# Cross-attention stage of a Perceiver layer: DMA order, the 65-row tile's sum, and the order of work at a step's end

## The reference, cut to what matters

```python
C_q  = layernorm(x) @ Wq_d;  C_kv = ctx @ Wkv_d          # 1601 keys of 32 latents per batch
scores = einsum('bnhl,bkl->bhnk', (C_q @ W_qk) by head, C_kv) / sqrt(32)
attn = softmax(scores);  V_up = C_kv @ Wv_u               # 16 heads of 32
x = x + einsum('bhnk,bkhd->bnhd', attn, V_up)
# beside it, for later blocks:
k_sel, v_sel = k_cache[block_idx], v_cache[block_idx]     # 16 of 128 blocks
coeff = mean(abs(w - mean_w))                             # for w1, w3 and w2
```

## Time and profile before

| | us |
|---|---|
| median of 3 runs | 1012.36 (1009.2 to 1012.99) |
| the profiled execution | 1013.66 |
| its span | 1011.9 |
| TensorE busy | 916.1 (91%) |
| VectorE, ScalarE, GpSimd busy | 619.5, 509.6, 384.4 |

### The profile page before, as it was taken

How to read it: one execution, slowest core, us unless ns; L and a number is a source line. 1 busy time by engine, 2 the same in 40 slices (tenths; PEclk the granted TensorE clock), 3 DMA queues, 4 the chain that set the end, 5 groups by cost and what they waited for, 6 DMA issues and landing times. The chain is left out here.

```text
span 1011.9 us, 15312 instructions
## 1 busy us (share of the span) xinstructions
PE 916.1 (91%) x5330; PEld 660.0 (65%) x5330; DVE 619.5 (61%) x994; ACT 509.6 (50%) x995; POOL 384.4 (38%) x256
## 2 busy tenths in 40 slices
PE   4748999999599897999999999999999997699997
PEld 2324454444344376888888888888888886578886
DVE  2444467556365154767757576775757675598783
ACT  2314566655455454645636364563636554255551
POOL 2024578656555502433423243342323332244430
PEclk9956999999699889999999999999999998889999
DMA  9475855534430062101101010110101000355531
GB/s 324 185 234 205 300 159 218 176 132 147 155 110 1 1 250 94 42 22 42 42 21 54 29 41 21 41 41 21 53 30 41 12 1 1 124 188 191 206 104 41
DMA packets 46178, 103.70 MB, mean 102 GB/s; under 512 B 11314, under 2 KB 16434, under 8 KB 45106
## 3 DMA queue, kind: packets, MB, share of 16 engines
q1 hardware_dynamic: 44754, 102.94, 29.6%
q10 hardware_dynamic: 1376, 0.13, 0.1%
HBM read 97.08 MB, written 1.05 MB: 97 GB/s over the span
## 5 line engine op out<-in xcount | busy, mean ns | idle before, releaser
L1324 POOL TENSOR_TENSOR head_probs<-head_probs,inverse_den 128x576 f32<-128x576 f32 x128 | 146.8, 1147 | 297.7 <-DVE inverse_den L1255 297.6
L806 DVE TENSOR_REDUCE max_part<-psum 128x1 f32<-128x804 f32 x128 | 121.4, 990 | 85.0 <-PE psum L608 84.9
L741 ACT ACTIVATE probs<-psum 128x512 f32<-128x512 f32 (+1 forms) x208 | 108.7, 600 | 51.3 <-PE psum L629 45.3
L1202 ACT ACTIVATE head_probs<-psum,neg_max 128x576 f32<-128x576 f32 x128 | 94.5, 738 | 76.7 <-PE psum L1093 43.1
L534 POOL TENSOR_TENSOR prob_sums<-probs 128x1024 f32<-128x1024 f32 x48 | 115.0, 2405 | 44.8 <-ACT probs L741 44.6
L1268 DVE TENSOR_REDUCE neg_max<-psum 128x1 f32<-128x576 f32 x128 | 96.2, 754 | 36.2 <-PE psum L1077 29.6
L608 PE MATMUL psum<-c_t,q_t 96*128 96x402 f32 x256 | 80.9, 405 | 19.7 <-DMA c_t<-c_high 13.9
L629 PE MATMUL psum<-q_t,c_t 97*128 97x512 f32 (+1 forms) x208 | 77.9, 448 | 19.6 <-ACT probs L741 18.1
L1248 DVE TENSOR_TENSOR probs_t_low<-psum,probs_t_high 128x512 fp32r<-128x512 f32 x128 | 87.5, 684 | 9.5 <-ACT probs_t_high L1208 8.4
L608 PEld LDWEIGHTS psum<-c_t,q_t 96*128 96x128 f32 x256 | 49.1, 211 | 62.1 <-DVE max_part L806 34.6
L1077 PE MATMUL psum<-k_high,query_t_high 128*128 (+1 forms) x256 | 84.2, 329 | 4.9 <-DVE query_t_low L1233 2.9
(11 more groups left out here) (161 smaller groups left out, 1909.8 us busy)
## 6 DMA issues: line engine op xcount, KB each, us to landing
cache<-in_ctx_dram SPq DMA_DIRECT2D x4, 3202.0 KB, 12.4
ctx_t_odd<-in_ctx_dram SPq DMA_DIRECT2D x4, 3202.0 KB, 14.3
w_raw<-in_L_ffn_w_dram SPq DMA_DIRECT2D x24, 448.0 KB, 5.1
w_raw<-in_L_ffn_mean_w_dram SPq DMA_DIRECT2D x24, 448.0 KB, 6.0
ffn_raw<-in_L_ffn_w_dram SPq DMA_DIRECT2D x42, 256.0 KB, 3.8
ffn_raw<-in_L_ffn_mean_w_dram SPq DMA_DIRECT2D x42, 256.0 KB, 4.1
wq_nat<-in_L_attn_wq_dram SPq DMA_DIRECT2D x32, 256.0 KB, 2.7
wo_nat<-in_L_attn_wo_dram SPq DMA_DIRECT2D x32, 256.0 KB, 2.6
```

Source lines behind the costliest of these rows:

```text
L741: act.activation(prob_buffer(b, t)[0:rows, half * BANK:(half + 1) * BANK], psum[0:rows, n % SCORE_BANKS, :], ACT.Exp, scale=XSCALE).then_i ...
L806: dve.tensor_reduce(max_part[:, qt, pair:pair + 1], psum[:, bank:bank + 2, 0:PIECE_KEYS], AX.XY, ALU.max).then_inc(s_max, 1)
L1202: act.activation(probs[:, qt, :].rearrange("p (a k) -> p a k", a=2), psum[:, 2 * (qt % 2):2 * (qt % 2) + 2, 0:HALF], ACT.Exp, bias=neg_max ...
L1324: pool.tensor_tensor(probs[:, qt, :], probs[:, qt, :], rden[:, qt:qt + 1].to_broadcast([P, KEYS]), ALU.mult).then_inc(s["norm"], 1)
```

## The change

The weight pieces get a semaphore for each of their three pairs, a load of pair i waits for the absolute sum of pair i alone, and a difference for its own pair. On SP, `place_keys(b)` stands ahead of the load of context b+2, and the cache gather behind the last pieces. GpSimd's `add_tail` adds the 65-row tile into the sixth sum, and the two matmuls on it go. `scores(b+1, 1)` stands ahead of `denominators(b)`, `scores(b, 3)` ahead of `mix(b-1)`, `copy_den` behind tile 1. The second and third absolute sum stand behind a step's last exponential. VectorE's addition to `x` (`add_mixed`) stands behind `negate_max`.

```diff
-ABS_AT = (3, 5, 7)
+ABS_AT = 3
...
-    s_raw = core.sem("w_raw_in", own)
+    s_raw = [core.sem(f"w_raw_in{i}", own) for i in range(3)]
...
-        return (g // KT) * ADDS + min((g % KT) // 2 + 1, ADDS) if g >= 0 else 0
+        return (g // KT) * (ADDS + 1) + (g % KT) // 2 + 1 if g >= 0 else 0
...
         @block.sync
-            def load_pieces(k):
-                wait(sp, s_abs, 3 * k)
-                for i, pair in enumerate(wnames):
-                    for j, n in enumerate(pair):
-                        sp.dma_start(w_raw[:, i, j, :], flat[n][:, k * PIECE:(k + 1) * PIECE]).then_inc(s_raw, 16)
+            def load_pieces(k, i):
+                wait(sp, s_abs, 3 * (k - 1) + i + 1)
+                for j, n in enumerate(wnames[i]):
+                    sp.dma_start(w_raw[:, i, j, :], flat[n][:, k * PIECE:(k + 1) * PIECE]).then_inc(s_raw[i], 16)
...
-            load_pieces(0)
+            for i in range(3):
+                load_pieces(0, i)
             sp.dma_start(index[:, :], arg["block_idx"].rearrange("(a k) -> a k", a=1)).then_inc(s_idx, 16)
             for b in range(BATCH):
+                if b > 2:
+                    load_pieces(b - 1, 1)
+                    load_pieces(b - 1, 2)
+                place_keys(b)
                 if b + 2 < BATCH:
                     sp.wait_ge(s_c, b + 1)
                     load_context(core, ctx_t, sp, b + 2, b % 2)
-                place_keys(b)
-                if b == BATCH - 2:
-                    sp.wait_ge(s_idx, 16)
-                    sp.wait_ge(s_c, BATCH - 1)
-                    gather_cache(core, sp, index)
-                if b > 0:
-                    load_pieces(b)
+                if b == 1:
+                    load_pieces(1, 0)
+                    load_pieces(1, 1)
+                    load_pieces(1, 2)
+                elif b > 1:
+                    load_pieces(b, 0)
+            load_pieces(BATCH - 1, 1)
+            load_pieces(BATCH - 1, 2)
+            sp.wait_ge(s_idx, 16)
+            gather_cache(core, sp, index)
...
         @block.gpsimd
-                pool.wait_ge(s_raw, 96 * (k + 1))
+                pool.wait_ge(s_raw[i], 32 * (k + 1))
...
+            def add_tail(b):
+                pool.wait_ge(s_exp, HALVES * (b + 1))
+                pool.wait_ge(s_add, (ADDS + 1) * b + ADDS)
+                pool.tensor_tensor(sums[ADDS - 1][0:TAIL, :], sums[ADDS - 1][0:TAIL, :],
+                                   prob_buffer(b, KT - 1)[0:TAIL, :], ALU.add).then_inc(s_add, 1)
...
                     add_pair(s, u)
                     if s == 0 and u == 0:
                         compressed_low(2)
+                add_tail(s)
                 if s + 3 < BATCH:
                     compressed_low(s + 3)
...
         @block.tensor
                 for k in range(ADDS // 2):
-                    pe.wait_ge(s_add, ADDS * b + 2 * k + 2)
+                    pe.wait_ge(s_add, (ADDS + 1) * b + (2 * k + 2 if k < ADDS // 2 - 1 else ADDS + 1))
...
-                for half in range(2):
-                    at = 2 * LKV * half + LKV
-                    mm = pe.matmul(psum[at:at + LKV, DEN_BANK, :], ones[0:TAIL, :],
-                                   prob_buffer(b, KT - 1)[0:TAIL, half * BANK:(half + 1) * BANK], start=False, stop=True)
                 mm.then_inc(s_den, 1)
...
                     scores(b, 2 * u + 2)
                     if lead:
                         max_scores(b + 1, 3 * u + 1 if u == 0 else 3 * u)
+                    if b == 0 and u == 0:
+                        compress(2)
+                    scores(b, 2 * u + 3)
                     if b > 0 and u == 0:
                         mix(b - 1)
-                    elif u == 0:
-                        compress(2)
-                    scores(b, 2 * u + 3)
...
                 if lead:
                     scores(b + 1, 0)
+                    scores(b + 1, 1)
                 denominators(b)
-                if lead:
-                    scores(b + 1, 1)
...
         @block.scalar
                         wait(act, s_add, pairs_summed(b, t))
-                        wait(act, s_den, tails_summed(b, t))
...
                     exponential(b, t)
-                    if t == 0 and b > 0:
+                    if t == 1 and b > 0:
                         copy_den(b - 1)
-                    if t in ABS_AT and b + 1 < BATCH:
-                        abs_sum(b + 1, ABS_AT.index(t))
+                    if t == ABS_AT and b + 1 < BATCH:
+                        abs_sum(b + 1, 0)
...
+                if b + 1 < BATCH:
+                    abs_sum(b + 1, 1)
+                    abs_sum(b + 1, 2)
                 if b + 3 < BATCH:
                     compressed(b + 3)
...
         @block.vector
                 mm.then_inc(s_mix, 1)
+
+            def add_mixed(b):
                 if b % 2:
                     dve.wait_ge(s_mix, b + 1)
...
                     negate_max(b + 1)
                 else:
                     update_x(b - 1)
+                if b > 0:
+                    add_mixed(b - 1)
                 if b + 3 < BATCH:
                     place_values(b + 3)
                 copy_u(b)
             update_x(BATCH - 1)
+            add_mixed(BATCH - 1)
```

More of the change, by code:

```diff
@@ L477, in pairs_summed @@
         g = KT * b + t - 4
-        return (g // KT) * ADDS + min((g % KT) // 2 + 1, ADDS) if g >= 0 else 0
-    def tails_summed(b, t):
-        g = KT * b + t - 4
-        return g // KT + 1 if g >= 0 and g % KT == KT - 1 else 0
+        return (g // KT) * (ADDS + 1) + (g % KT) // 2 + 1 if g >= 0 else 0
     with nc.Block() as block:
@@ L658, in denominators @@
                             at = 2 * LKV * half + LKV * odd
-                            pe.matmul(psum[at:at + LKV, DEN_BANK, :], ones[:, :],
-                                      sums[2 * k + odd][:, half * BANK:(half + 1) * BANK],
-                                      start=(k == 0), stop=(k == ADDS // 2 - 1 and odd == 0))
-                for half in range(2):
-                    at = 2 * LKV * half + LKV
-                    mm = pe.matmul(psum[at:at + LKV, DEN_BANK, :], ones[0:TAIL, :],
-                                   prob_buffer(b, KT - 1)[0:TAIL, half * BANK:(half + 1) * BANK], start=False, stop=True)
+                            mm = pe.matmul(psum[at:at + LKV, DEN_BANK, :], ones[:, :],
+                                           sums[2 * k + odd][:, half * BANK:(half + 1) * BANK],
+                                           start=(k == 0), stop=(k == ADDS // 2 - 1))
                 mm.then_inc(s_den, 1)
```

## The result

The changed kernel takes 977.51 us (median of 4 runs, 974.57 to 979.48), the kernel before, in the runs beside it, 1010.78 us (1008.8 to 1012.99). The ratio is 0.967 (95%: 0.963 to 0.971). Predicted were 981.5 us and a range of 975 to 990, which holds it. The profiled execution took 976.39 us, its span 974.6; before it was 1013.66 and 1011.9.

What follows compares the result with a forecast made beforehand. TensorE, 91% busy, was taken as the bound, with its waits and slow clock open to gain. 6.3 + 7.4 + 1.2 + 3.1 + 14.0 - 0.5 - 0.2 = 31.3 us gave 981.5 us, range 975 to 990.

Steps and rivals of the forecast that it cites:

- Part 1: Stage start: place_keys(0) ahead of context 2 brings the first max scores earlier, gain 6.3 us.
- Part 2: Start of each step: tile matmuls gone and scores 1 ahead of the sums, 1.05 us seven times, gain 7.4 us.
- part 3: Mid-step: GpSimd gets the denominators earlier, so its lag in steps 1 and 3 goes, gain 1.2 us.
- Part 4: Addition to x moved to a step's end: TensorE's wait for VectorE in steps 2, 4 and 6 goes, gain 3.1 us.
- Part 5: GpSimd's add_tail: one more instruction of 2.4 us a step, on the path only at step 7's end, cost 0.5 us.
- Part 6: Gather behind the pieces: the stall and slow clock in step 5 go, gain 14.0 us.
- Part 7: Two absolute sums behind the last exponential: 0.1 us each in steps 5 and 6, cost 0.2 us.
- Rival B: Step 7 stays at full clock despite its wait, some 3 us more gain, 978.5 us; chance 0.11.
- A: Start of each step: copy_den behind tile 1 eats the gain of the new order, 989 us; chance 0.12.
- D: Slower: the clock falls at a new wait and stays down within the step, 1034 us with four; chance 0.02.
- E: Pieces for step 5 still come late, as a load waits for a sum at a step's end, 995.5 us; chance 0.02.
- C: New waits drop the clock at the start of steps 1 to 6, 4.1 us each, 1006 us; chance 0.03.

Runs made afterwards that it cites:

- context_first: Changed kernel with the load of context b+2 ahead of place_keys(b) again; 985.84 us, ratio 0.977.
- tail_on_pe: Changed kernel without add_tail, the two matmuls on the 65-row tile back in the denominators on TensorE; 981.59 us, ratio 0.972.
- old_start: Changed kernel with scores 1 behind the denominators and copy_den behind tile 0 again; 985.17 us, ratio 0.975.
- gather_alone: Kernel before with one edit, the cache gather moved behind the last piece; 995.06 us, ratio 0.985.
- copy_den_t0: Changed kernel with only copy_den back behind tile 0, scores 1 still ahead of the denominators; 995.75 us, ratio 0.985.
- x_in_step: Changed kernel with the addition to x back within the step, behind update_x; 1004.28 us, ratio 0.993.
- gather_back: Changed kernel with the gather back behind place_keys(6), ahead of the loads of piece 6; 988.08 us, ratio 0.979.
- abs_in_step: Changed kernel with the absolute sums back behind tiles 3, 5 and 7; 977.40 us, ratio 0.968.
- two_queues: Changed kernel with the 15 transfers of place_keys(0) shared, 7 on ScalarE's queue and 8 on SP's; 971.93 us, ratio 0.962.

## Why the prediction was right, point by point

**The sum** held, 33.3 us by the medians for 31.3, but several of its terms have other sizes and one another cause than I gave. That the total came so close is partly luck: clock that the sum had not counted on gave some 5 us in the two profiles, and the medians, with a faster before than the 1012.36 us that I started from, show 4 us less gain than the profiles.

*Part 1, the start: right.* 6.0 us by the interval against context_first, 6.6 by the wait against before, where 6.3 was taken. From the last issue to the first max scores it took 55.17 - 53.39 = 1.78 us, for my 1.9 and 0.15; no row shows the 0.15 by itself. The other 0.7 of the table's 7.3 lies ahead of it, and step 0 gives 0.7 back by its clock, which I had not counted.

*Part 2, the step's start: mis-sized.* Max 1 at 5.73 us was nearly the predicted 5.65, and the two new waits are there, 0.22 and 0.29 us for the predicted 0.4. But "1.05 us a step, seven times" fails twice. The 65-row tile is worth 0.84 us (tail_on_pe), the order 0.94 (old_start), together 1.78, which is what steps 1 and 3 gained (32.11 - 30.34 = 1.77). Of the order's 0.94 at most 0.2 is the earlier max 1; the rest is *part 3*, GpSimd's lag. I gave that 0.59 us in steps 1 and 3 alone, because only there it shows in before; in steps 2 and 4, as I read it, the wait for VectorE covered it. In step 7, where no max scores follow, part 2 brought half of its 1.05 us. The long wait ends 295.01 - 288.69 = 6.32 us after scores 0, in before 327.13 - 320.94 = 6.19: ScalarE sets that point, and it now does tile 1 ahead of `copy_den`. But the scores behind it are those of tile 3 now and were those of tile 2. Against gather_alone, whose clock held in step 7 too, TensorE is 0.57 us ahead by the last tiles, 306.50 - 287.53 = 18.97 us behind the shift row for 325.99 - 306.45 = 19.54. After, then gather_alone:

```profile
306.50 0.50 PE L639 MATMUL psum<-q_t,c_t 97*128 97x512 f32 x1 [0.22 <-ACT probs L745]
```

```profile
325.99 0.50 PE L628 MATMUL psum<-q_t,c_t 97*128 97x512 f32 x1 [0.22 <-ACT probs L740]
```

*Part 4, the addition to x: length right, worth mis-sized.* It takes 2.47 us at the step's end and TensorE doesn't see it. Steps 2 and 4 gained 2.35 and 2.37 us, so beside the 1.78 only 0.57 to 0.59 each is left for it, not 1.03. What the sum missed is its price if left in place, 26.8 us: I priced the edits one by one against the GpSimd of before.

*Part 5, `add_tail`: right in place, a little dearer.* TensorE waits 0.61 us for it at the stage's end. Against gather_alone the last `copy_den` starts 0.16 us later behind the shift row (26.53 us for 26.37) although the tiles came 0.57 earlier, so the tail's sum costs 0.73 us for the 0.5 taken. A 65-row sum takes 2.38 us beside 2.39 for 128 rows: rows don't count. Whether VectorE would do the tail in some 1.2 us, an estimate from the ratio in the Trainium skill (GPSIMD Engine Reference, "Elementwise — side-by-side cycle accounting"), wasn't tried.

*Part 6, the gather: right in place, 0.6 us too large.* 13.4 us in step 5 (gather_alone) for 14.0. I priced step 5 without its stall as step 6 less 1.03 us, and that subtraction was wrong. Two edits weren't tried alone: the semaphores by pair (gather_alone has no stall in step 5 without them) and `mix` behind scores 3.

*Part 7: right*, zero for 0.2.

*Rival B* came. The profiled run of after, 976.39 us, lies 6.0 below the 982.4 forecast for it: 1.9 of that in step 7, 2.6 in later stages, the rest in small sums of both signs in the table. Step 7's gain of 2.4 us is all clock: against gather_alone, whose clock also held, after's step 7 is 0.17 us longer (0.57 won by the order, 0.73 paid for the tail). *A, D and E* didn't come. *C*'s mechanism showed in copy_den_t0. The 2.6 us outside the stage are mostly clock too: in before TensorE did 52 matmuls from 847.6 to 863.6 us at a clock of 0.79 (gather_alone has 0.74 there), in after 62 in the same stretch behind the stage's end, from 812.9 to 828.9 us, at 1.00. Why the clock fell in the one and not in the other stays open. The later stages take 654.8 to 658.7 us in the twelve profiles.

## What to carry to other kernels

Look for what stands behind a long run of issues in a strictly ordered queue before looking at any engine: moving 32 gather transfers was 13 of 33 us. Price an edit against the engines as the other edits leave them: moving the addition to x was worth under 2 us by the steps of the old kernel and 27 in the new one. And where a wait of about 1 us stands in a stream that is otherwise dense, shorten it even if it looks cheap, since it can take the clock with it; it does not always.

## What the runs showed of the hardware that was not expected

- VectorE's addition with two SBUF inputs can be shut out by several GpSimd instructions in a row: 7.14 to 7.16 us three times in x_in_step, for 0.69 alone. In before it got its turn behind the first of such a row, 2.4 us, three times as well. What decides stays open.
- A wait of 1.02 to 1.07 us in step 7 is sometimes followed by a stretch at 1.2 GHz and sometimes not. In the profiles of before, context_first, tail_on_pe and old_start it was (step 7 of 33.85, 33.39, 36.54 and 32.98 us), in those of after, gather_back, gather_alone, abs_in_step and two_queues it was not (31.24 to 31.42 us), nor in that of x_in_step, whose step 7 took 32.22 us by a slow stretch only at its end. The waits cover the same 1.02 to 1.07 us in both groups. Price: 1.6 to 5 us. What decides it stays open. In steps 1 to 6 with no wait above 0.7 us the clock stayed at 1.00 in all twelve profiles, and so it did in the six steps of before and gather_alone with a wait of 1.02 to 1.04 us; behind the 1.14 us of copy_den_t0 it fell in three steps of six.
